# Direct combine on TensorE for the last 8 of 32 expert units, with paired PSUM evictions

## The reference, cut to what matters

```
x = x + xattn(layernorm(x), ctx_512, ...)
h = layernorm(x)                                   # 512 rows of 256
scores = sigmoid(h @ gate_weight.T)                # 512 x 32
topk_idx = top 4 experts of the 2 best of 4 groups, by scores + bias
topk_w = scores[topk_idx] / sum * 2.5
routed = sum over experts e of combine[:, e] * ((silu(h @ w1[e].T) * (h @ w3[e].T)) @ w2[e].T)
shared = (silu(h @ ws1.T) * (h @ ws3.T)) @ ws2.T
return x + routed + shared
```

## Time and profile before

| what | value |
| --- | --- |
| median of 3 runs | 354.38 us (353.24 to 356.27) |
| the profiled execution's own time | 356.48 us |
| its span, from the first to the last instruction | 354.6 us |
| mean granted TensorE clock | 0.918 |
| TensorE busy | 276.0 us (78% of the span) |
| VectorE busy | 230.6 us (65%) |
| ScalarE busy | 170.9 us (48%) |
| GpSimd busy | 139.0 us (39%) |

### The profile page before, as it was taken

How to read it: one execution, slowest core, us unless ns; L and a number is a source line. 1 busy time by engine, 2 the same in 40 slices (tenths; PEclk the granted TensorE clock), 3 DMA queues, 4 the chain that set the end, 5 groups by cost and what they waited for, 6 DMA issues and landing times.

```text
span 354.6 us, 5403 instructions
## 1 busy us (share of the span) xinstructions
PE 276.0 (78%) x1671; PEld 200.8 (57%) x1671; DVE 230.6 (65%) x574; ACT 170.9 (48%) x403; POOL 139.0 (39%) x126
## 2 busy tenths in 40 slices
PE   3858769898898998989998989578277999996000
PEld 3644538776587775877666878444234666663000
DVE  4294853789897898968988598558722454454133
ACT  3342855767687786786866465440012333330000
POOL 0550921987009691076920000000275445400672
PEclk9998998999999999999999999978758999999555
DMA  7910006000150000600008974310032444422242
GB/s 264 389 63 0 3 19 219 2 0 0 42 198 2 2 0 4 221 2 0 0 2 283 404 293 149 119 59 1 16 104 83 140 138 148 151 91 91 77 135 84
DMA packets 17595, 35.41 MB, mean 100 GB/s; under 512 B 2848, under 2 KB 10272, under 8 KB 17568
## 3 DMA queue, kind: packets, MB, share of 16 engines
q1 hardware_dynamic: 15264, 28.77, 23.0%
q0 software_dynamic: 2304, 6.29, 6.2%
HBM read 29.81 MB, written 5.24 MB: 99 GB/s over the span
## 4 chain that ended last, share of the span: by engine, by line
PE 48%; DVE 19%; issue 7%; ACT 6%; POOL 4%; DMA 1%; another core or an unknown queue 1%; POOLq 0%; ACTq 0%; DVEq 0%
PE bank L561 8%; PE bank L510 6%; PE bank L495 5%; PE bank L579 4%; PE bank L467 4%; POOL ctT L1118 4%; DVE nmax L851 3%; PE bank L445 2%; DVE pT L864 2%; PE bank L487 2%; PE bank L486 2%; PE bank L552 2%; PE bank L392 2%; PE bank L394 2%; PE bank L393 2%
## 5 line engine op out<-in xcount | busy, mean ns | idle before, releaser
L1113 POOL DMA_INDIRECT rope<-xn_rows,idx x32 | 30.4, 950 | 98.2 <-DVE idx L1019 74.7
L305 POOL TENSOR_TENSOR rtmp<-abuf,rope 128x512 f32<-128x512 f32 x22 | 29.2, 1326 | 75.6 <-issue 58.1
L851 DVE TENSOR_REDUCE nmax<-bank 128x1 f32<-128x512 f32 x64 | 43.4, 681 | 15.1 <-PE bank L487 14.1
L714 ACT ACTIVATE prob<-bank,nmax 128x512 f32<-128x512 f32 x48 | 33.0, 689 | 30.2 <-DVE nmax L851 29.7
L864 DVE TENSOR_TENSOR pT<-bank,pT 128x512 fp32r<-128x512 f32 x64 | 43.5, 681 | 1.9 <-ACT pT L722 1.9
L722 ACT CAST pT<-bank 128x512 fp32r<-128x512 f32 x64 | 37.6, 590 | 6.7 <-PE bank L495 6.3
L510 PE MATMUL bank<-pT,kvs 128*128 128x256 f32 x256 | 38.3, 292 | 0.8 <-DVE pT L864 0.6
L495 PE MATMUL bank<-ident,prob 128*128 128x128 f32 x192 | 29.5, 278 | 6.2 <-DVE pT L864 5.5
L561 PE MATMUL bank<-wall,nmat 128*64 (+1 forms) x256 | 34.2, 414 | 0.0
L510 PEld LDWEIGHTS bank<-pT,kvs 128*128 128x128 f32 x256 | 32.5, 190 | 2.2 <-issue 1.0
L495 PEld LDWEIGHTS bank<-ident,prob 128*128 128x128 f32 x192 | 23.1, 142 | 17.6 <-DVE prob L859 10.0
(11 more groups left out here) (175 smaller groups left out, 516.7 us busy)
## 6 DMA issues: line engine op xcount, KB each, us to landing
wall<-in_w_exp SPq DMA_DIRECT2D x32, 384.0 KB, 6.9
y_rows<-nmat SPq DMA_DIRECT2D x32, 128.0 KB
wring<-in_w_attn SPq DMA_DIRECT2D x16, 224.0 KB, 4.2
wring<-in_w_attn SPq DMA_DIRECT2D x4, 640.0 KB, 8.1
wring<-in_w_attn SPq DMA_DIRECT2D x4, 512.0 KB, 6.8
rope<-in_rope_q SPq DMA_DIRECT2D x1, 768.0 KB, 6.6
x_sb<-in_x SPq DMA_DIRECT2D x1, 512.0 KB, 3.5
xn_rows<-xn SPq DMA_DIRECT2D x4, 128.0 KB, 1.8
```

What stands on the lines that cost most here:

```text
L714: act.activation(probs[t % 4], s_ps[t % 3][:, :], ACT.Exp, bias=nmax[:, t:t + 1], accum_out=psum_e[:, t:t + 1]).then_inc(s_exp, 1)
L851: dve.tensor_reduce(nmax[:, t:t + 1], s_ps[t % 3][:, :], AX.X, ALU.max, negate=True).then_inc(s_max, 1)
L1113: pool.indirect_dma_start(xg[:, u % XG, :], None, xn_dram, bass.IndirectOffsetOnAxis(idx[:, 1, u:u + 1], 0)) \
```

## The change: what it does

The last 8 units (24 to 31, `DIR = 8`, `NG_U = 24`) no longer go through y_rows. VectorE multiplies each row of their output in PSUM with the weight of its slot, once rounded to fp32r and once for the remainder (`weighted_rows`, two buffers of halves in a ring of four), and TensorE multiplies a one-hot (slot by token) with both halves and adds all 8 units into two banks for the 512 tokens (`combine`: 8 products a unit). The weights of the slots come from 32 small products (`slot_weights`, in TensorE's turn 2), whose one-hots VectorE makes between `top_weights` and `places` (`weight_ones`). The one-hots of tokens (`hot_row`) are one comparison of 128x512 for each direct unit, in VectorE's turns 4 to 11, against a table of 256 KB that SP loads before its last expert loads. The 16 gathers remain, now waiting for units 0 to 23 alone; choices that lie in a direct unit get weight 0 and the last row of y_rows, by two more operations in `places`. Each gather has a semaphore of its own, the additions of the first token tile stand in VectorE's last but one turn (16), and every tile gets an addition from the PSUM sums.

Two units now share one bank for their row transposes and one for their g transposes, with one copy for both on ScalarE and VectorE. That frees banks 4 and 7 for the sums.

```diff
@@ -46,6 +46,9 @@
 NX = E + 1
 BLK = 64
 NU = E
+DIR = 8
+NG_U = NU - DIR
+YD = 4
 XG, XS, YS, GS = 6, 4, 4, 4
 NK = TT * TOPK
 C_LT, C_ONE, C_IOTA, C_PAD, C_VAL, C_TS, C_TI, C_END = 0, P, P + E, P + E + BLK, P + 2 * E + BLK, P + 2 * E + BLK + NK, \
...
@@ -153,9 +158,11 @@
         eo_ps = bank[4][0:E, 0:E]
         cnt_ps = bank[7][0:E, 0:E]
         inv_ps = bank[7][:, E:E + NU]
-        xt_ps = bank[3:5]
+        xt_ps = bank[3]
         hu_ps = bank[0:2]
-        gt_ps = bank[6:8]
+        gt_ps = bank[6]
+        acc_ps = (bank[4], bank[7])
+        sw_ps = bank[7][:, D:D + DIR]
         yu_ps = (bank[2], bank[5])
 
 
@@ -205,6 +212,11 @@
         su = kv_flat[:, 0:2 * I].rearrange("p (r n) -> p r n", r=2)
         gu = kv_flat[:, 2 * I:4 * I].rearrange("p (r n) -> p r n", r=2)
         gTu = ctmp[:, :, :].rearrange("p a s -> p (a s)")[:, 0:GS * P].rearrange("p (r n) -> p r n", r=GS)
+        one_hot = pT[:, :, :, :, :].rearrange("p a b c s -> p (a b c s)")[:, 0:DIR * T].rearrange("p (u t) -> p u t", u=DIR)
+        yd = xnT[:, :, :, :].rearrange("p a d t -> p (a d t)")[:, 0:YD * 2 * D].rearrange("p (r a d) -> p r a d", r=YD, a=2)
+        tokens = rt_flat[:, 2 * T:3 * T]
+        w_st, w_ov = (ct_flat[:, 6 * T + n * NK * DIR:6 * T + (n + 1) * NK * DIR].rearrange("p (i e) -> p i e", e=DIR)
+                      for n in range(2))
         y4 = ctT[:, :, :].rearrange("p n t -> p (n t)").rearrange("p (t k d) -> p t k d", t=TT, k=TOPK)
         iota_over = moe[:, C_OV:C_END]
         lower, ones_e, iota_b = moe[:, C_LT:C_ONE], moe[:, C_ONE:C_IOTA], moe[:, C_IOTA:C_PAD]
@@ -229,7 +241,7 @@
         d_ws = sem("d_ws")
         d_sh = sem("d_sh"); d_moe = sem("d_moe"); d_xn = [sem(f"d_xn{i}") for i in range(TT)]
         d_xg = [sem(f"d_xg{i}") for i in range(XG)]; d_yu = [sem(f"d_yu{i}") for i in range(YS)]
-        d_y4 = [sem(f"d_y4{i}") for i in range(TT)]
+        d_y4 = [sem(f"d_y4{i}") for i in range(TT * TOPK)]
         d_out = sem("d_out")
         chain_v = sem("chain_v")
         chain_p = sem("chain_p")
...
@@ -370,13 +384,14 @@
                 load_expert(held)
                 held += 1
             sp.wait_ge(s_mm, TILES)
+            sp.dma_start(tokens, iota_t).then_inc(d_iota, 16)
             while held < E:
                 load_expert(held)
                 held += 1
             for tt in range(TT):
                 sp.wait_ge(x2_n, tt + 1)
                 sp.dma_start(xn_dram[tt * P:(tt + 1) * P, :], xn[:, tt, :]).then_inc(d_xn[tt], 16)
-            for u in range(NU):
+            for u in range(NG_U):
                 sp.wait_ge(yu_ev, u + 1)
                 sp.dma_start(y_dram[u * P:(u + 1) * P, :], yu[:, u % YS, :]).then_inc(d_yu[u % YS], 16)
             for tt in range(TT):
@@ -546,10 +561,10 @@
 
             def x_rows(u):
                 pe.wait_ge(d_xg[u % XG], 16 * (u // XG + 1))
-                if u >= 2:
-                    pe.wait_ge(xt_ev, u - 1)
+                if u >= 2 and u % 2 == 0:
+                    pe.wait_ge(xt_ev, u)
                 for dc in range(ND):
-                    mm = pe.transpose(xt_ps[u % 2][:, dc * P:(dc + 1) * P], xg[:, u % XG, dc * P:(dc + 1) * P], ident[:, :])
+                    mm = pe.transpose(xt_ps[:, (u % 2 * ND + dc) * P:(u % 2 * ND + dc + 1) * P], xg[:, u % XG, dc * P:(dc + 1) * P], ident[:, :])
                 mm.then_inc(xt_mm, 1)
 
             def hidden(u):
@@ -565,9 +580,9 @@
 
             def g_rows(u):
                 pe.wait_ge(gu_done, u + 1)
-                if u >= 2:
-                    pe.wait_ge(gt_ev, u - 1)
-                pe.transpose(gt_ps[u % 2][:, 0:P], gu[:, u % 2, :], ident[:, :]).then_inc(gt_mm, 1)
+                if u >= 2 and u % 2 == 0:
+                    pe.wait_ge(gt_ev, u)
+                pe.transpose(gt_ps[:, (u % 2) * P:(u % 2 + 1) * P], gu[:, u % 2, :], ident[:, :]).then_inc(gt_mm, 1)
 
             def out_rows(u):
                 pe.wait_ge(gt_ev, u + 1)
@@ -578,6 +593,24 @@
                 for s, w in enumerate((over_w[u], u * WE)):
                     pe.matmul(yu_ps[u % 2][s * BLK:(s + 1) * BLK, 0:D], gTu[:, u % GS, s * BLK:(s + 1) * BLK],
                               wall[:, bass.ds(w + 2 * ND * I, D)], start=True, stop=True).then_inc(yu_mm, 1)
+
+            def slot_weights():
+                pe.wait_ge(w_one, 2)
+                for k in range(NK):
+                    for s, one in enumerate((w_ov, w_st)):
+                        mm = pe.matmul(sw_ps[s * BLK:(s + 1) * BLK, :], one_r[:, k, :], one[:, k, :], start=(k == 0), stop=(k == NK - 1))
+                        if k == NK - 1:
+                            mm.then_inc(sw_mm, 1)
+
+            def combine(u):
+                pe.wait_ge(yu_ev, NG_U + u + 1)
+                pe.wait_ge(oh_done, u + 1)
+                for hl in range(2):
+                    for tt in range(TT):
+                        mm = pe.matmul(acc_ps[tt // 2][:, (tt % 2) * D:(tt % 2 + 1) * D], one_hot[:, u, tt * P:(tt + 1) * P],
+                                       yd[:, u % YD, hl, :], start=(u == 0 and hl == 0 and tt % 2 == 0),
+                                       stop=(u == DIR - 1 and hl == 1 and tt % 2 == 1), skip_group_check=True)
+                mm.then_inc(acc_mm, 1)
 
             def shared_hidden(w, signal):
                 for dc in range(ND):
@@ -640,17 +673,22 @@
                         mm.then_inc(inv_mm, 1)
 
             pe.wait_ge(d_ws, 16 * E)
-            for j in range(NU // 2 + 2):
+            for j in range(NU // 2 + 3):
                 if j < NU // 2:
                     x_rows(2 * j)
                     x_rows(2 * j + 1)
-                if j >= 2:
+                if 2 <= j < NU // 2 + 2:
                     g_rows(2 * j - 4)
                     g_rows(2 * j - 3)
                 if 1 <= j <= NU // 2:
                     hidden(2 * j - 2)
                     hidden(2 * j - 1)
-                if j >= 2:
+                if j == 2:
+                    slot_weights()
+                if 2 * j - 6 >= NG_U:
+                    combine(2 * j - 6 - NG_U)
+                    combine(2 * j - 5 - NG_U)
+                if 2 <= j < NU // 2 + 2:
                     out_rows(2 * j - 4)
                     out_rows(2 * j - 3)
 
@@ -762,10 +800,10 @@
             act.wait_ge(sh3_mm, 1)
 
             def x_evict(u):
-                act.wait_ge(xt_mm, u + 1)
+                act.wait_ge(xt_mm, u + 2)
                 if u >= XS:
-                    act.wait_ge(hu_mm, 2 * (u - XS) + 2)
-                act.copy(xTu[:, u % XS, :, :], xt_ps[u % 2][:, 0:ND * P].rearrange("p (d q) -> p d q", d=ND)).then_inc(xt_ev, 1)
+                    act.wait_ge(hu_mm, 2 * (u + 1 - XS) + 2)
+                act.copy(xTu[:, u % XS:u % XS + 2, :, :].rearrange("p r d q -> p (r d q)"), xt_ps[:, :]).then_inc(xt_ev, 2)
 
             def silu(u):
                 act.wait_ge(hu_mm, 2 * u + 2)
@@ -776,7 +814,6 @@
             for j in range(NU // 2 + 1):
                 if j < NU // 2:
                     x_evict(2 * j)
-                    x_evict(2 * j + 1)
                 if j >= 1:
                     silu(2 * j - 2)
                     silu(2 * j - 1)
@@ -1009,7 +1046,43 @@
                 link(dve.tensor_scalar(placef[:, 2, :], pickr[:, 1, :], -float(BLK), float(P // BLK), ALU.add, ALU.mult))
                 link(dve.scalar_tensor_tensor(row, pick[:, :].rearrange("p (t k) -> p t k", t=TT), 4096.0, row, ALU.is_lt, ALU.mult))
                 link(dve.tensor_tensor(home, home, row, ALU.add))
-                dve.tensor_tensor(place[:, 1, :], placef[:, 1, :], pickr[:, 0, :], ALU.add).then_inc(placed, 1)
+                link(dve.tensor_tensor(placef[:, 1, :], placef[:, 1, :], pickr[:, 0, :], ALU.add))
+                link(dve.scalar_tensor_tensor(topw[:, 0, :, :].rearrange("p t k -> p (t k)"), placef[:, 1, :], float(NG_U * P),
+                                              topw[:, 1, :, :].rearrange("p t k -> p (t k)"), ALU.is_lt, ALU.mult))
+                dve.tensor_scalar(place[:, 1, :], placef[:, 1, :], float(NG_U * P - 1), None, ALU.min).then_inc(placed, 1)
+
+            def weight_ones():
+
+                tw = topw[:, 1, :, :].rearrange("p t k -> p (t k)")
+                link(dve.scalar_tensor_tensor(vals[:, :], pick[:, :], 4096.0, tw, ALU.is_ge, ALU.mult))
+                dve.tensor_tensor(w_st, eq_v.rearrange("p (i e) -> p i e", e=E)[:, :, NG_U:NU],
+                                  vals[:, :].unsqueeze(2).to_broadcast([P, NK, DIR]), ALU.mult).then_inc(w_one, 1)
+                link(dve.tensor_tensor(w_ov, iota_over[:, NG_U:NU].unsqueeze(1).to_broadcast([P, NK, DIR]),
+                                       pickr[:, 1, :].unsqueeze(2).to_broadcast([P, NK, DIR]), ALU.is_equal))
+                dve.tensor_tensor(w_ov, w_ov, tw.unsqueeze(2).to_broadcast([P, NK, DIR]), ALU.mult).then_inc(w_one, 1)
+                link(dve.tensor_copy(tokf[:, :], idx[:, 1, NG_U:NU]))
+
+            def hot_row(u):
+                if u == 0:
```

(62 more changed lines are left out.)

11 lines of the change are left out of this document (8 added, 3 removed).

## The result

The changed kernel takes 364.86 us (median of 4 runs, 363.62 to 365.59), the kernel before in the same comparison 353.81. The ratio is 1.0275, with a 95% interval of 1.0226 to 1.0324: slower, where 345.1 was forecast. The span is 363.2 us, at a mean granted clock of 0.927. TensorE is busy for 293.4 us (81%), VectorE 240.0 (66%), ScalarE 169.7 (47%), GpSimd 140.0 (39%).

What follows compares the result with a forecast made beforehand. TensorE was taken to bound the loop, GpSimd's gathers the tail. VectorE's serial end at 344.0 plus 1.3 delay gave 345.3 against span 354.6, -9.3; from median 354.38, 345.1 us, range 340.5 to 350.5.

Steps and rivals of the forecast that it cites:

- Gathers begin at unit 23: Tail: sixteen gathers start at 316.7 on the old clock, last lands at 338.3, gather path ends at 341.4.
- the gathers don't start early: Rival at the tail: something holds GpSimd until the loop's end, giving 363; chance 0.02.
- The delay s: Loop up to unit 23: 32 slot-weight products in the third turn delay it by 1.3 us, ends -0.6 and 2.6.
- The paired evictions: Loop's PSUM copies: two units sharing a bank and one copy neither save nor cost time; zero.
- The lock: Rival in eight turns: VectorE's hot rows and GpSimd's gathers block each other, 3 us, median 348.1; chance 0.07.
- The combine: TensorE's additions at the end: eight fp32r products a unit, 1.05 us, or 2.1 a pair.
- The rival by which it costs its record: TensorE's end: 2.26 us a unit at full clock, or the same at the 1.2 GHz level; median 352.5, chance 0.10.
- VectorE's tail: End: weighting 0.95 us a unit, then serial token-tile additions; last combine at 335.2, output write at 344.0.
- What would show it wrong: Three signs: a middle turn above 4 us, a combine over 1.5, VectorE's last wait for TensorE's sums above 1.

Runs made afterwards that it cites:

- the spare gathers: Kernel before plus a third gather in each of eight middle turns, 128 rows into a buffer nobody reads: 362.48 us, 1.0152.
- the paced kernel: Changed kernel, its 16 gathers paced by TensorE's progress, two at a time, last six after the eighth combine, token-tile additions behind the loop: 351.62 us, 0.9893.

## Why the prediction was wrong, by its own steps

**Gathers begin at unit 23: this step failed.** It took GpSimd's gathers as work that lies beside TensorE at no cost, because GpSimd was free. The first part held: the first gather started at 320.16 against 318.0 forecast, sixteen at 1.25 us, the last landing near 341.6. But a row of sixteen holds back the engines that wait for TensorE: they are let go at 337.21, while the fourteenth runs, and at 342 to 343, behind the last. That moved the last combine's end from about 338.7 to 354.87. The sentence "the loop over units is TensorE's, the tail is GpSimd's" was true of the kernel before and said nothing of the two at once; no row of the trace showed more than two gathers in a row beside a full TensorE, except one place: the first turns. The prediction read there that "VectorE's wait there, 3.71 us, is on something that the profile cannot name", used it for the size of s, and didn't ask whether the same thing would meet sixteen gathers. With the spare gathers at +1.05 us a turn, the moved stall behind six and the wait gone where the gathers are paced, that wait has a cause, and carried over to the tail it would have given a slower rival with the right mechanism. The rival "the gathers don't start early" came near in time, 363, but by luck: nothing held GpSimd.

**The delay s** was about 3.5 us, above the 2.6 of its upper end. The step reckoned the slot weights as 2.62 us that fill an idle of 1.88. In turn 6 they cost 1.82 us, so the products are cheaper than thought; in turn 2 they stand in the stall and are stretched over 5.2 us. So the term was mis-sized, and by the trace for the same reason as above; the medians with the weights in turn 6 (1.0224 against 1.0275) don't tell it from noise.

**The paired evictions** at zero: right (0.998 [0.9947, 1.0013]). **The lock**: the eight hot rows took 476 to 478 ns, none near the 1.40 us of its worst case, so its 3 us are refuted. It is GpSimd that waits. Six token gathers begin while a hot row runs; they take 0.99 to 1.09 us, where all others from 262 us on take 0.94 or 0.95, and each ends 0.81 or 0.82 us after its hot row has ended. One of them, its hot row, and the gather behind:

```profile
292.28 0.48 DVE L1068 TENSOR_SCALAR pT<-rtmp,tokf 128x512 fp32r<-128x512 f32 x1
292.49 1.08 POOL L1195 DMA_INDIRECT rope<-xn_rows,idx  x1 [1.35 <-PE bank L567]
293.88 0.94 POOL L1195 DMA_INDIRECT rope<-xn_rows,idx  x1 [0.30 <-issue]
```

The Trainium skill (SBUF — State Buffer, section "SBUF: two separate sides") would have the gathers held by such operations, and the trace agrees, by at most 0.15 us a gather and at no cost in time. The same section says of the two sides: "A DMA cannot be slowed by a compute op, and vice versa." The transfers from SP and the plain ones from GpSimd agree (TensorE 28.00 of 28 us). With a third indirect gather in a turn TensorE has 23.96 of 28; as the bytes make no difference, this need not be at the two sides of which the sentence speaks.

**The combine** at 2.1 us a pair: 2.16 to 2.19 where nothing disturbs. The rival by which it costs its record, 4.5 a pair, is refuted for the full clock. Its other half came true for units 26 and 27: in the kernel after their combines took 2.08 us each (at 338.27 and 343.18), where the granted clock had fallen to 0.50, the level of 1.2 GHz (337 to 345.5 us), against 2.17 for the two in the paced kernel. That is a consequence of the stall, about 2 us of it. **VectorE's tail**: a weighted unit is 0.48 + 0.48 against 0.95, and from the last combine to the end there were 8.3 us against 8.8. In the kernel after, its additions no longer wait for gathers, since all had landed long before.

**What would show it wrong**: the middle turns stayed at 3.55 to 3.64 us, and VectorE had no wait for TensorE's sums at the end; its long waits stood ahead of the combines. Of the three signs only the combine of over 1.5 us showed, for the two units above.

The versions with paced gathers show what the idea is worth: 1.1% by pacing the tail, 1.7% with the slot weights in turn 6 as well, 2.2% with the start put right too. The forecast of 2.6% had the size of that, for a kernel that wasn't this one.

## What to carry to other kernels

Work that a free engine could do beside the bound one is not free until a row shows the two together at that density; here the price was 16 us for sixteen indirect gathers from GpSimd, and pacing them in pairs by TensorE's own semaphores removed it. A pace must leave the buffers ahead: conditions one unit tighter starved TensorE by 3.8 to 4.9 us at a time. And a wait in the trace of before that has no name is a price to be explained, or else carried to every place where the change makes the same surroundings.

## What the runs showed of the hardware that was not expected

Indirect gathers of GpSimd close together, beside dense products, delay what waits for TensorE. Two in a turn of 3.55 us leave TensorE at 10.00 of 10; a third makes the turn 4.6 us; six in a row made waits of 4.47 and 1.96 us, sixteen such of 3.05, 10.79, 3.90 and 16.87 us. All but the first of these end with the last gathers of their row or up to 3.1 us behind them. Rows of 1 KB or 64 bytes, 128 or 32 rows, registers or fixed addresses make no difference (ratios 1.015 to 1.020); the same bytes from SP or as a plain DMA from GpSimd cost nothing (1.0 and 1.0006).

Open: whether the products themselves or only the news of their completion are late. The records of the combines' products lie at 323.22 to 325.4, and the waits for TensorE's outputs of that time end at 337.21 and later, and ScalarE is let go 12 us after the last hidden product's record, which speaks for the news; but the ends of products are modelled in such a profile, and in the turns with a third gather TensorE's own rows have gaps of issue. Open too is what in the chip carries the effect, and how many gathers in a row are borne: between two and three for a turn of 3.55 us is all that was tried.

Smaller, and at no cost here: a comparison of 128x512 from SBUF to SBUF on VectorE holds a gather that begins while it runs, which then ends 0.81 or 0.82 us after it, 0.99 to 1.09 us long in place of 0.94 or 0.95.
